# The shared expert of the two-choice stage, two batches to a product

## The chip, the cores and the metric

The kernel runs on one core of a Trainium2 chip. The metric is the device time of one execution, in microseconds. A core has five engines that run their own instruction streams and meet at semaphores: PE (TensorE, matmuls into PSUM; PEld is its loading of weights), ACT (ScalarE), DVE (VectorE), POOL (GpSimd) and SP, which here only issues DMAs. PSUM has eight banks, each of 128 partitions by 512 float32 values.

## What is computed

The program is a chain of attention and feed-forward layers, each followed by a layer norm, on 8 batches of 256 tokens of 128 values. The change lies in one of them: a mixture of eight experts of which each token takes two, beside a shared expert that all tokens go through. From the reference, cut:

```python
# x: (8, 256, 128); eight routed experts of inner width 512, a shared one of 1024
xg = xf[dispatch]                                   # each expert's tokens, at most 320
gate = silu(einsum('ech,ehi->eci', xg, rg)); up = einsum('ech,ehi->eci', xg, ru)
eout = einsum('eci,eih->ech', gate * up, rd)
routed = zeros_like(xf).at[dispatch.reshape(-1)].add(contrib.reshape(-1, h))
shared = jax.nn.silu(x @ sg) * (x @ su) @ sd
return shared + SCALE * routed.reshape(b, s, h)
# and around it: x = layernorm(x + that)
```

## The kernel before

The stage is `stage_top2_experts`, L2543. Constants: `B` is 8 batches, `L` 256 tokens a batch, `TPB` 2 tiles of 128 tokens a batch, `NT` 16 tiles in all, `SC` 8 chunks of 128 hidden columns of the shared expert, `FC` 4 chunks of a routed expert, `E2` 8 experts, `C2` 320 places each.

Order of the stage. DVE works out the routing. POOL then issues 32 indirect DMAs (L2830) that scatter the token rows into slots in memory; when all have landed, SP loads the slots (L2846) and PE turns them (L2628). While this goes on, PE, ACT and DVE compute the first half of the shared expert, batches 0 to 3. Next come the eight routed experts; their results are stored, and POOL issues 32 indirect DMAs (L2838) that gather two rows per token. Meanwhile the engines compute the second half of the shared expert, batches 4 to 7, and DVE combines, batch by batch, the two gathered rows and the shared result (`combine`, L2779 to L2788), then normalises (L2799). At the end PE turns the tokens again (L2649) and ACT writes them to `xT` (L2685).

One batch of the shared expert goes chunk by chunk. PE computes the gate product (`sg`) and the up product (`su`) of 256 tokens, L2618; in float32 each product is two matmul records. ACT takes the silu of the gate (L2674), DVE multiplies it with the up product into `shared_hid` (L2762). Gate products alternate between banks 3 and 4, up products between 5 and 6, so PE may be two chunks ahead of DVE; chunks 0 and 1 of a batch wait for the last product of DVE of the batch before. After chunk 1 of batch i PE computes the down products of batch i-1 (L2609: 8 chunks for each of two tiles, and L2610, which adds `x` by a product with the identity) into bank 7; 18 products, 36 matmul records. ACT copies bank 7 to `shared` (L2666, `keep_shared`) behind its silu of chunk 1. The last batch of a half has its down products at the end of the half.

The order of work on each engine is the order in which the code is written. The first half's last copy is what the turning of the slots waits behind, on ACT; the second half's last copy is what the last `combine` waits for.

## Time and profile before

| | us |
|---|---|
| median of 3 runs | 1851.13 (1848.86 to 1851.44) |
| profiled execution | 1853.07 |
| its span | 1851.2 |
| PE busy | 1537.6 (83%) |
| DVE busy | 1013.3 (55%) |
| ACT busy | 868.2 (47%) |
| POOL busy | 632.8 (34%) |

The page also cuts the span in 40 slices of 46.3 us and gives the busy share of each engine in each, and the clock that was granted to PE. The stage of this document lies in slices 31 to 36, from about 1384 to 1629 us. Times in the rows count from the start of the span. In a row of the timeline, the square brackets hold how long the engine had been idle before it, and what ended that. A row of PE shows when the matmul started, while its semaphore is raised when it has ended.

### The profile page before, as it was taken

The page shows a single profiled execution, that of the slowest core. Times are in us where ns is not written, and L with a number is a line of the kernel's source. Part 1 is how long each engine was busy: PE and PEld are TensorE (multiplying, and loading weights), DVE is VectorE, ACT ScalarE, POOL GpSimd, SP SyncE. Part 2 cuts the span into 40 slices and gives each one's busy share as a digit, 9 for nine tenths or more (in the row PEclk, how much of TensorE's full clock was granted, in tenths as well). Part 3 has the DMA queues.
Part 4 walks back from the last instruction along what each step waited for, and adds up shares of the span by engine and source line. Part 5 has one row for each costly group of instructions (what it writes and reads, how often), then busy time and mean ns, then how long its engine had stood idle before and what let it go on. Part 6 is the DMA issues. An engine that isn't in the chain of part 4 may idle for free. (4 is left out here: it accounts for less than half of the span.)

```text
span 1851.2 us, 31581 instructions
## 1 busy us (share of the span) xinstructions
PE 1537.6 (83%) x11326; PEld 1136.8 (61%) x11327; DVE 1013.3 (55%) x2402; ACT 868.2 (47%) x1935; POOL 632.8 (34%) x707
## 2 busy tenths in 40 slices
PE   4689977899787999995669999999974895668996
PEld 3356664566573577764647878787763774535664
DVE  6565546665376799982245553566452221344555
ACT  5556544555357777752434444444441231235553
POOL 3487513976132577753210001000036005111113
PEclk8799988899896899996869999999986898869998
DMA  7300000000002444706160000000001102100000
GB/s 221 102 13 12 12 7 3 12 18 12 7 1 38 80 75 78 79 22 165 42 186 1 1 1 1 1 1 0 1 1 46 29 19 46 11 4 2 2 2 24
DMA packets 75277, 63.71 MB, mean 34 GB/s; under 512 B 25367, under 2 KB 62790, under 8 KB 75142
## 3 DMA queue, kind: packets, MB, share of 16 engines
q1 hardware_dynamic: 65142, 53.53, 13.0%
q0 software_dynamic: 3072, 6.30, 1.7%
q10 hardware_dynamic: 6928, 2.12, 0.5%
q8 instruction: 81, 1.33, 0.3%
q14 instruction: 54, 0.44, 0.1%
HBM read 48.09 MB, written 9.57 MB: 31 GB/s over the span
## 5 line engine op out<-in xcount | busy, mean ns | idle before, releaser
L1354 POOL TENSOR_TENSOR inject<-delta_x,b_rows 128x512 f32<-128x512 f32 x128 | 159.6, 1270 | 82.7 <-DVE delta_x L1604 42.2
L1625 DVE TENSOR_TENSOR_SCAN state<-bank,inject 128x512 f32<-128x512 f32 x128 | 150.4, 1206 | 5.0 <-ACT bank L1535 4.7
L2058 POOL TENSOR_TENSOR ve<-mv,eps 128x1 f32<-128x1 f32 x32 | 6.1, 190 | 341.3 <-DVE mv L2206 341.3
L1535 ACT ACTIVATE bank<-delta,a_neg 128x255 f32<-128x255 f32 x256 | 109.0, 472 | 11.9 <-DVE state L1625 11.4
L3313 DVE TENSOR_REDUCE top<-bank 128x2 f32<-128x512 f32 (+1 forms) x96 | 61.8, 686 | 72.4 <-PE bank L3015 51.5
L2167 ACT ACTIVATE Z<-bank 128x512 f32<-128x512 f32 x64 | 34.7, 595 | 129.4 <-PE bank L2120 129.4
L2762 DVE TENSOR_TENSOR shared_hid<-shared_gate,bank 128x256 f32<-128x256 f32 x64 | 26.5, 421 | 124.9 <-ACT shared_gate L2674 72.6
L2144 ACT ACTIVATE U<-bank 128x512 f32<-128x512 f32 x128 | 74.6, 593 | 40.3 <-PE bank L2081 39.2
L2618 PE MATMUL bank<-xT,sg 128*128 128x256 f32 x128 | 45.3, 437 | 55.8 <-DVE shared_hid L2762 51.3
L594 POOL TENSOR_TENSOR rotated<-rot_cos,rot_sin 128x512 f32<-128x512 f32 x56 | 70.8, 1268 | 52.2 <-DVE rot_sin L900 52.2
L600 POOL TENSOR_TENSOR inv_norm<-sum_sq,neghalf 128x16 f32<-128x16 f32 x28 | 82.0, 2929 | 4.2 <-POOL sum_sq L598 0.2
L1440 PEld LDWEIGHTS bank<-tabs,by_token 128*128 128x128 f32 x512 | 67.5, 195 | 24.9 <-issue 15.0
L637 PE MATMUL bank<-wqkv,hT 128*128 128x512 f32 x128 | 69.1, 670 | 15.0 <-ACT hT L798 12.0
L1546 ACT ACTIVATE by_token<-bank,c_cols 128x256 f32<-128x256 f32 x128 | 53.6, 469 | 50.1 <-PE bank L1411 49.8
L1444 PE MATMUL bank<-x_work,tabs 128*128 128x512 f32 x128 | 73.7, 658 | 0.0
L3226 ACT ACTIVATE prob<-bank 128x384 f32<-128x384 f32 x128 | 53.2, 501 | 37.0 <-PE bank L3043 37.0
L1440 PE MATMUL bank<-tabs,by_token 128*128 128x128 f32 x512 | 68.9, 278 | 0.0
L2618 PEld LDWEIGHTS bank<-xT,sg 128*128 128x128 f32 x128 | 24.7, 214 | 68.2 <-DVE shared_hid L2762 56.6
L897 DVE TENSOR_TENSOR rot_cos<-bank,rope 128x512 f32<-128x512 f32 x64 | 43.8, 685 | 39.9 <-ACT squares L803 29.1
L803 ACT ACTIVATE squares<-bank 128x512 f32<-128x512 f32 x64 | 38.0, 598 | 43.4 <-PE bank L637 25.4
L605 POOL TENSOR_TENSOR rotated<-rotated,inv_norm 128x512 f32<-128x512 f32 x56 | 57.2, 1042 | 2.2
L825 ACT ACTIVATE prob<-bank 128x512 f32<-128x512 f32 x64 | 34.7, 595 | 44.6 <-PE bank L684 44.6
(564 smaller groups left out, 4205.1 us busy)
## 6 DMA issues: line engine op xcount, KB each, us to landing
b_rows<-b_rows_dram SPq DMA_DIRECT2D x32, 512.0 KB, 8.6
v<-v SPq DMA_DIRECT2D x32, 130.0 KB, 2.3
slots<-zero SPq DMA_DIRECT2D x10, 256.0 KB, 3.6
rows<-slots SPq DMA_DIRECT2D x10, 256.0 KB, 4.7
moe_w<-in_L_ffn_rg_dram SPq DMA_DIRECT2D x1, 2048.0 KB, 8.6
moe_w<-in_L_ffn_ru_dram SPq DMA_DIRECT2D x1, 2048.0 KB, 14.3
wqkv<-in_L_ffn_wqkv_dram SPq DMA_DIRECT2D x2, 768.0 KB
slots_out<-y SPq DMA_DIRECT2D x8, 160.0 KB, 2.1
```

The source lines that it names most:

```text
L594: pool.tensor_tensor(rot[:, p, m, :], rc[:, m % 2, :], rs[:, m % 2, :], ALU.add).then_inc(s.added.sem, 1)
L600: pool.tensor_tensor(flat(rn), flat(ss), net.neghalf[:, 0:2 * LH], ALU.pow).then_inc(s.inv_norm.sem, 2)
L605: pool.tensor_tensor(r, r, rn[:, m, :].unsqueeze(2).to_broadcast([P, LH, LDH]), ALU.mult).then_inc(s.roped.sem, 1)
L637: pe.matmul(to, hT[:, p, tok(t)], w[:, j * INNER:(j + 1) * INNER], start=True, stop=True).then_inc(s.qk_ps.sem, 1)
L1354: pool.tensor_tensor(dB[:, n % R, :, :], dx[:, :, seq(n)], both(b_all[:, q % 4, n % CH, :]), ALU.mult).then_inc(s.inject.sem, 1)
L1440: last = pe.matmul(sum_bank(i)[:, c * L + t * P:c * L + (t + 1) * P], hcT[:, j % RT, t, c * P:(c + 1) * P], ident, start=(k == 0 and t == ...
L1444: last = pe.matmul(sum_bank(i)[:, :], ident, flat(hc[:, j % R, :, :]), start=False, stop=(k == NS - 1))
L1535: last = act.activation(dA[n % RD][:, c, 1:L], delta[:, c, i * L + 1:(i + 1) * L], ACT.Exp, scale=a_neg[:, c, k:k + 1])
L1625: dve.tensor_tensor_scan(flat(h[:, n % R, :, :]), flat(dA[n % RD]), flat(dB[:, n % R, :, :]), 0.0, ALU.mult, ALU.add).then_inc(s.state.sem, 1)
L2144: act.activation(U[:, m % 2, 4 * (g - 1):4 * g, :], bank[n % 2][:, :].rearrange("p (h t) -> p h t", h=4), ACT.Copy)\
L2618: pe.matmul(to[:, 0:L], w[:, c * P:(c + 1) * P], net.xT[:, i * L:(i + 1) * L], start=True, stop=True).then_inc(done.sem, 1)
L3313: dve.tensor_reduce(to, M[u % 2].rearrange("p (c k) -> p c k", c=count), AX.X, ALU.max).then_inc(s.maxed.sem, 1)
```

## The change

The shared expert is computed by pairs of batches. A gate or up product takes 512 tokens, and fills a whole bank; ACT and DVE treat 512 columns in an instruction. `shared_gate` and `shared_hid` are twice as wide. The down products of a pair are computed together, after chunk 1 of the next pair: the even batch's into bank 0, the odd one's into bank 7, and ACT copies both one after the other. DVE no longer runs `combine` between single batches but three of them behind the first pair of the second half and four behind the second. A wait is added ahead of the turning of the slots, since that writes bank 0 too.

```diff
-        sgate, shid = sb("shared_gate", [P, 2, L]), sb("shared_hid", [P, 2, SC, L])
+        sgate, shid = sb("shared_gate", [P, 2, 2 * L]), sb("shared_hid", [P, 2, SC, 2 * L])
...
+            shared_bank = lambda i: bank[7 * (i % 2)]
...
-                def shared_down(i):
-                    pe.wait_ge(s.s_hid.sem, s.s_hid.at(i, SC))
-                    pe.wait_ge(s.shared.sem, s.shared.at(i, 0))
-                    for t in range(TPB):
-                        tok = slice(t * P, (t + 1) * P)
-                        for c in range(SC):
-                            pe.matmul(bank[7][:, tok], shid[:, i % 2, c, tok], net.sd[:, c, :], start=(c == 0), stop=False)
-                        last = pe.matmul(bank[7][:, tok], net.xT[:, i * L + t * P:i * L + (t + 1) * P], net.tab("ident"), start=False, stop=True)
-                    last.then_inc(s.shared_ps.sem, 1)
+                def shared_down(p):
+                    pe.wait_ge(s.s_hid.sem, s.s_hid.at(p, SC))
+                    for i in (2 * p, 2 * p + 1):
+                        if i >= 2:
+                            pe.wait_ge(s.shared.sem, s.shared.at(i - 1, 0))
+                        for t in range(TPB):
+                            tok, at = slice(t * P, (t + 1) * P), i % 2 * L + t * P
+                            for c in range(SC):
+                                pe.matmul(shared_bank(i)[:, tok], shid[:, p % 2, c, at:at + P], net.sd[:, c, :], start=(c == 0), stop=False)
+                            last = pe.matmul(shared_bank(i)[:, tok], net.xT[:, i * L + t * P:i * L + (t + 1) * P], net.tab("ident"), start=False, stop=True)
+                        last.then_inc(s.shared_ps.sem, 1)
...
-                                pe.matmul(to[:, 0:L], w[:, c * P:(c + 1) * P], net.xT[:, i * L:(i + 1) * L], start=True, stop=True).then_inc(done.sem, 1)
+                                pe.matmul(to[:, :], w[:, c * P:(c + 1) * P], net.xT[:, 2 * i * L:2 * (i + 1) * L], start=True, stop=True).then_inc(done.sem, 1)
...
-                shared_expert(0, HALF)
+                shared_expert(0, PAIRS // 2)
+                pe.wait_ge(s.shared.sem, s.shared.at(PAIRS - 2, 1))
...
-                            act.activation(sgate[:, c % 2, :], gate_bank(c)[:, 0:L], ACT.Silu).then_inc(s.s_silu.sem, 1)
+                            act.activation(sgate[:, c % 2, :], gate_bank(c)[:, :], ACT.Silu).then_inc(s.s_silu.sem, 1)
                             if c == 1 and i > first:
-                                keep_shared(i - 1)
+                                keep_shared(2 * i - 2)
+                                keep_shared(2 * i - 1)
...
-                dve.tensor_tensor(shid[:, i % 2, c, :], sgate[:, c % 2, :], up_bank(c)[:, 0:L], ALU.mult).then_inc(s.s_hid.sem, 1)
+                dve.tensor_tensor(shid[:, i % 2, c, :], sgate[:, c % 2, :], up_bank(c)[:, :], ALU.mult).then_inc(s.s_hid.sem, 1)
```

On PE, around the first down products of the first half. Before, the down products of batch 0 stand behind chunk 1 of batch 1, and chunk 2 of batch 1 follows:

```order
L2618 MATMUL bank4<-xT,sg 128x256
L2618 MATMUL bank6<-xT,su 128x256
L2609 MATMUL bank7<-sd,shared_hid_246 128x128 x8
L2610 MATMUL bank7<-tabs,xT 128x128
L2609 MATMUL bank7<-sd,shared_hid_246 128x128 x8
L2610 MATMUL bank7<-tabs,xT 128x128
L2618 MATMUL bank3<-xT,sg 128x256
L2618 MATMUL bank5<-xT,su 128x256
```

With the change, chunk 1 of pair 1 is followed by the down products of batches 0 and 1:

```order
L2621 MATMUL bank4<-xT,sg 128x512
L2621 MATMUL bank6<-xT,su 128x512
L2612 MATMUL bank0<-sd,shared_hid_246 128x128 x8
L2613 MATMUL bank0<-tabs,xT 128x128
L2612 MATMUL bank0<-sd,shared_hid_246 128x128 x8
L2613 MATMUL bank0<-tabs,xT 128x128
L2612 MATMUL bank7<-sd,shared_hid_246 128x128 x8
L2613 MATMUL bank7<-tabs,xT 128x128
L2612 MATMUL bank7<-sd,shared_hid_246 128x128 x8
L2613 MATMUL bank7<-tabs,xT 128x128
L2621 MATMUL bank3<-xT,sg 128x512
```

Half as many gate and up products stand ahead of the first down products for the same tokens, and twice as many down products stand together.

On ACT, the first half; `shared_gate` is written by the silu, `shared` by `keep_shared`:

```order
-L2674 ACTIVATE shared_gate<-bank 128x256 x10
-L2666 ACTIVATE shared<-bank 128x256
-L2674 ACTIVATE shared_gate<-bank 128x256 x8
-L2666 ACTIVATE shared<-bank 128x256
-L2674 ACTIVATE shared_gate<-bank 128x256 x8
-L2666 ACTIVATE shared<-bank 128x256
-L2674 ACTIVATE shared_gate<-bank 128x256 x6
-L2666 ACTIVATE shared<-bank 128x256
```

```order
+L2678 ACTIVATE shared_gate<-bank 128x512 x10
+L2670 ACTIVATE shared<-bank 128x256 x2
+L2678 ACTIVATE shared_gate<-bank 128x512 x6
+L2670 ACTIVATE shared<-bank 128x256 x2
```

The first copy stands behind ten silus as before, but these are of pairs now, so it stands behind 5120 columns instead of 2560.

## Rows read from the trace of the kernel before

**Rows 1.** Stretches: us, busy us (instructions) of each engine, PE's clock, DMA share, GB/s.

```profile
1409.00:1440.00 31.00, 6.84 (x18) 3.49 (x17) 0.78 (x3) 0.94 (x3) 18.99 (x20) 0.59 0.25 77
1440.00:1445.00 5.00, 4.88 (x12) 3.89 (x13) 1.24 (x4) 0.97 (x3) 0.00 (x0) 0.50 0.21 60
...
1549.00:1586.00 37.00, 4.37 (x30) 3.54 (x28) 0.34 (x2) 0.19 (x1) 23.65 (x26) 0.62 0.41 46
```

**Rows 2.** Timeline of POOL, first and last scatter and gather: start, us, line, operation [idle].

```profile
1393.57 1.07 POOL L2830 DMA_INDIRECT slots<-x_tok,scatter  x1 [4.98 <-DVEq L2742]
...
1432.83 0.96 POOL L2830 DMA_INDIRECT slots<-x_tok,scatter  x1 [0.30 <-issue]
1540.59 0.98 POOL L2838 DMA_INDIRECT y_first<-slots_out,gather  x1 [106.80 <-DMA slots_out<-y]
...
1579.33 0.94 POOL L2838 DMA_INDIRECT y_second<-slots_out,gather  x1 [0.30 <-issue]
```

**Rows 3.** Timeline of ACT, silus of batch 1, and the copies behind both holes.

```profile
1404.99 0.38 ACT L2674 ACTIVATE shared_gate<-bank 128x256 f32<-128x256 f32 x1 [1.53 <-PE bank L2618]
1407.14 0.38 ACT L2674 ACTIVATE shared_gate<-bank 128x256 f32<-128x256 f32 x1 [1.77 <-issue]
1438.95 0.38 ACT L2666 ACTIVATE shared<-bank 128x256 f32<-128x256 f32 x1 [31.43 <-remote]
...
1585.81 0.38 ACT L2666 ACTIVATE shared<-bank 128x256 f32<-128x256 f32 x1 [38.46 <-remote]
```

**Rows 4.** Timeline of PE in the first half, 1405 to 1428 us.

```profile
1405.92 1.95 PE L2609 MATMUL bank<-sd,shared_hid 128*128 128x128 f32 x16
...
1411.35 0.27 PE L2609 MATMUL bank<-sd,shared_hid 128*128 128x128 f32 x1 [1.63 <-issue]
...
1414.18 0.29 PE L2610 MATMUL bank<-tabs,xT 128*128 128x128 f32 x1 [1.63 <-issue]
...
1427.57 0.59 PE L2618 MATMUL bank<-xT,su 128*128 128x256 f32 x1 [1.51 <-issue]
```

**Rows 5.** Timeline of PE in the second half, the last down products of batch 4.

```profile
1551.00 0.39 PE L2610 MATMUL bank<-tabs,xT 128*128 128x128 f32 x2
```

**Rows 6.** Timeline of ACT and PE in the stage of one-choice experts, during its scatters.

```profile
868.81 0.60 ACT L1808 ACTIVATE la_k<-bank 128x512 f32<-128x512 f32 x1 [6.47 <-remote]
...
870.94 2.66 PE L1793 MATMUL bank<-la_p,y 64*128 64x128 f32 x14 [0.34 <-issue]
```

**Rows 7.** Timeline of ACT, the last copy of each half.

```profile
1474.68 0.38 ACT L2666 ACTIVATE shared<-bank 128x256 f32<-128x256 f32 x1 [4.90 <-PE bank L2610]
...
1621.48 0.38 ACT L2666 ACTIVATE shared<-bank 128x256 f32<-128x256 f32 x1 [0.72 <-PE bank L2610]
```

**Rows 8.** Timeline of PE in steady state, batches 2 and 3.

```profile
1448.66 1.95 PE L2609 MATMUL bank<-sd,shared_hid 128*128 128x128 f32 x16
...
1452.68 0.60 PE L2618 MATMUL bank<-xT,sg 128*128 128x256 f32 x2
...
1457.43 0.59 PE L2618 MATMUL bank<-xT,su 128*128 128x256 f32 x2
1458.59 0.70 PE L2618 MATMUL bank<-xT,sg 128*128 128x256 f32 x2 [0.57 <-DVE shared_hid L2762]
```

**Rows 9.** Durations in ns (min/median/max) of PE, and groups by form: busy us, mean ns.

```profile
L637 PE MATMUL bank<-wqkv,hT x60: 592/592/1192, 61.1 to 194.4; 128*128 128x512 f32 x60
...
L2618 PE MATMUL bank<-xT,sg x128: 376/379/797, 1389.9 to 1615.8; 128*128 128x256 f32 x128
...
L897 DVE TENSOR_TENSOR rot_cos<-bank,rope 128x512 f32<-128x512 f32 x64 | 43.8, 685 | 39.9 <-ACT squares L803 29.1
...
L825 ACT ACTIVATE prob<-bank 128x512 f32<-128x512 f32 x64 | 34.7, 595 | 44.6 <-PE bank L684 44.6
```

**Rows 10.** Timeline of DVE, the first normalisation of the stage's end.

```profile
1621.07 2.14 DVE L2799 TENSOR_SCALAR y_second<-y_first,n_mv,n_rstd 128x128 f32<-128x128 f32 x8
```

**Rows 11.** DMA queues from 1402 to 1404 us: packets, MB, share of the engines' time.

```profile
q8 instruction: 1, 0.02, 3.1%
```

More of the change, by code:

```diff
@@ L2564, in stage_top2_experts @@
         SC = IS // P
-        sgate, shid = sb("shared_gate", [P, 2, L]), sb("shared_hid", [P, 2, SC, L])
+        sgate, shid = sb("shared_gate", [P, 2, 2 * L]), sb("shared_hid", [P, 2, SC, 2 * L])
         shared = sb("shared", [P, NT, D])
-        HALF, EARLY = B // 2, B - 1
+        PAIRS, EARLY = B // 2, B - 1
         MS = [(0, P), (P, P), (2 * P, C2 - 2 * P)]
@@ L2642, in _ @@
                 pe.wait_ge(s.y_sb.sem, s.y_sb.at(0, E2))
-                shared_expert(HALF, B)
+                shared_expert(PAIRS // 2, PAIRS)
                 for i in range(B):
@@ L2665, in keep_shared @@
                     act.wait_ge(s.shared_ps.sem, s.shared_ps.at(i, 1))
-                    act.activation(shared[:, TPB * i:TPB * (i + 1), :], bank[7][:, 0:L].rearrange("p (t d) -> p t d", d=D), ACT.Copy)\
+                    act.activation(shared[:, TPB * i:TPB * (i + 1), :], shared_bank(i)[:, 0:L].rearrange("p (t d) -> p t d", d=D), ACT.Copy)\
                         .then_inc(s.shared.sem, 1)
@@ L2685, in update @@
                     act.activation(net.xT[:, i * L:(i + 1) * L], bank[1 + i % 2][:, 0:L], ACT.Identity).then_inc(s.x_updated.sem, 1)
-                shared_expert(0, HALF)
-                keep_shared(HALF - 1)
+                shared_expert(0, PAIRS // 2)
+                keep_shared(PAIRS - 2)
+                keep_shared(PAIRS - 1)
                 for g in range(KT // 4):
@@ L2701, in _ @@
                 copy_y(act, E2 - 1)
-                shared_expert(HALF, B)
+                shared_expert(PAIRS // 2, PAIRS)
+                keep_shared(B - 2)
                 deviation(0, 0, EARLY)
@@ L2754, in _, with shared_pair @@
                 weights()
-                def shared_batch(i):
+                def shared_pair(i):
                     for c in range(SC):
@@ L2760, in shared_batch @@
                         if i >= 2:
-                            dve.wait_ge(s.shared_ps.sem, s.shared_ps.at(i - 1, 0))
-                        dve.tensor_tensor(shid[:, i % 2, c, :], sgate[:, c % 2, :], up_bank(c)[:, 0:L], ALU.mult).then_inc(s.s_hid.sem, 1)
-                for i in range(HALF):
-                    shared_batch(i)
+                            dve.wait_ge(s.shared_ps.sem, s.shared_ps.at(2 * (i - 1), 0))
+                        dve.tensor_tensor(shid[:, i % 2, c, :], sgate[:, c % 2, :], up_bank(c)[:, :], ALU.mult).then_inc(s.s_hid.sem, 1)
+                for i in range(PAIRS // 2):
+                    shared_pair(i)
                 for e in range(E2):
@@ L2800, in normalise @@
                     last.then_inc(s.xn_ready.sem, 1)
-                shared_batch(HALF)
-                combine(0)
-                shared_batch(HALF + 1)
-                combine(1)
-                combine(2)
-                shared_batch(HALF + 2)
-                combine(3)
-                combine(4)
-                shared_batch(HALF + 3)
-                combine(5)
-                combine(6)
+                shared_pair(PAIRS // 2)
+                for i in range(3):
+                    combine(i)
+                shared_pair(PAIRS // 2 + 1)
+                for i in range(3, EARLY):
+                    combine(i)
                 inverse(0, 0, EARLY)
```

## The prediction

> **What bounds the kernel now.** I read the page first: PE is busy for 83% of the span, but the fortieths between about 1410 and 1435 us and between about 1550 and 1585 us are almost empty on PE, and both lie in the stage that the change edits. The table of stretches then gives the size of the two holes: 6.84 us of PE work in 31 us, and 4.37 us in 37 us, on a granted clock of 0.59 and 0.62 [rows 1]. Third I asked who works in them. It is POOL alone, with its indirect DMAs: the 32 scatters run from 1393.57 to 1433.8 us, the 32 gathers from 1540.59 to 1580.3 us [rows 2]. Fourth, the timelines of ACT and PE show what waits. In the first half PE ran the down products of batch 0 from 1405.92 on, at full pace; then, from 1411.35, one matmul in one or two microseconds, the last of that group at 1414.18, and after the gate and up products of chunks 2 and 3 of batch 1 it stopped at 1427.57 [rows 4]. ACT waits for exactly the semaphore of the matmul at 1414.18 (its copy of bank 7, line 2666), and gets it at 1438.95 [rows 3]: 24 us late. In the second half the matmul that ACT waits for starts at 1551.00 [rows 5], and ACT gets the signal at 1585.81 [rows 3]. The profile calls the releaser "remote", since the matmul had ended long before. So while POOL issues indirect DMAs, PE's signals arrive late and PE itself is slowed. The first routed stage shows the same at another place: PE is back at full pace at 870.94, when its 16 scatters are over, and ACT's wait before it reads "remote" too, 6.47 us long [rows 6].
>
> I call this the hold, and its end the release: 1438.95 and 1585.81 us, 5.2 and 5.5 us after the last indirect DMA was issued. What each half is worth is then what is left after the release, up to ACT's last copy at 1474.68 and at 1621.48 [rows 7]: 35.7 us in both halves. Everything before the release is hidden under POOL's DMAs, and everything after it is on the path, since routed experts follow the first half and the last normalisation the second.
>
> **The pieces, part by part.** A chunk is one of the 8 pieces of 128 hidden columns. (1) Products. In steady state six chunks of a batch run from 1452.68 to 1457.43, start to start 0.43 us for a gate or up product of 256 columns, so 0.86 a chunk [rows 8]. Each product is two matmul records; a record of 512 columns takes 592 ns where one of 256 takes 379 [rows 9], 213 ns more, as much as the 215 ns pace. So a chunk of a pair costs 1.72 us, and two batches cost PE what they did: half as many matmuls, no time saved in the stream. (2) ACT and DVE per chunk: 0.60 and 0.69 us for 512 columns [rows 9], together 1.3, under the 1.72 of PE; both engines have cover, and their 32 saved instructions each are worth nothing on the path. (3) The gap at the end of a batch, where PE waits for the last product of DVE: its last pair of matmuls starts at 1457.43, the next possible start is 0.43 later, and the real one is at 1458.59 [rows 8]: 0.73 us. With 512 columns it grows by the longer DVE instruction, 0.27, to 1.0. Eight gaps of 0.73 become four of 1.0: 1.8 us saved in all. (4) Down products: 4.02 us a batch, 1448.66 to 1452.68 [rows 8]; unchanged in number, now two batches in a row, 8.04, into banks 0 and 7. PE's wait for ACT's copy of two batches ago is met long before. ACT copies both while PE goes on to chunk 2, whose first product needs 0.86 us; nothing waits. The new wait ahead of the transposes is for the copy of batch 2, four microseconds older than the end of the down products: free. (5) DVE combines batches 0, 1 and 2 after pair 2, three times 1.7 us, under 11 us of PE work; batches 3 to 6 after pair 3, 6.7 us under 8.04 of down products. The last normalisation started at 1621.07 [rows 10], 0.4 ahead of the last copy. Now four combines follow the last product of DVE, which ends 8.3 before that copy; 6.7 for them (eight short instructions each, taken at 1.7) and 0.7 for root and reciprocal make it start 0.9 ahead. Gain 0.5 us, between 0 and 1.
>
> Add the pieces up for before, as a test: resume 1.2, 20 chunks 17.2, three gaps 2.2, three downs 12.1, the last copy 0.2; and PE restarts at half clock, 0.50 over the first 5 us [rows 1], which costs 2.5. Sum 35.4 of 35.7: the model holds, 0.3 unexplained.
>
> **Where the gain comes from.** The order of PE's work against the hold changes. Before, the release finds done: batch 0, chunks 0 to 3 of batch 1, one batch of down products. After, PE starts pair 0 at 1389.9, as now, without the idle time at 1394 (its two chunks last until ACT's table load is over). Slow clock until some 1394.6, chunks 2 to 7 by 1407.1, chunks 0 and 1 of pair 1 by 1411.5, and only then the dense down products, 72 matmuls. In the second half pair 2 starts at 1537.6 as now; its chunks end at 1551.4, those of pair 3 that come first at 1555.7. In the hold PE got 33 of 36 down matmuls through at full pace and then 11 matmuls from 1411.35 to 1427.57, 0.68 a microsecond. Applied to 72: 33 by 1415, 13 more until 1434, 26 left over, 2.9 us; the second half the same within 0.2. Left after a release: 2.9 of down products, six chunks 10.3, one gap 1.0, two downs 8.0, copy 0.2, slow clock 2.5, the unexplained 0.3: 25.2 against 35.7. The change gains 10.5 us a half, 21.0, and 0.5 in the tail: **21.5 us**. In plain words: per matmul issued, PE gets twice the columns through before it is slowed, and what it does while slowed are down products that no one needs yet.
>
> Bounds of the unknown: how many of the 72 get through. None, if the hold stops PE at once: 8.0 left instead of 2.9, gain 5.4 a half. All: 0 left, gain 13.4 a half. Main case 1824 to 1841. I stay near the middle since the rate is one read in the same code under the same DMAs.
>
> The profiled execution took 1853.07 us for its span of 1851.2, and the median of the runs is 1851.13; the differences above are taken from the median: 1851.1 - 21.5 = 1829.6, **1830 us**.
>
> **Rivals.** (a) The hold strikes early and hard. In the first half ACT's start at 1404.99 is the last on time; that of 1407.14 stood 1.77 us [rows 3]. The changed kernel is then in chunk 6 of pair 0. If from there on no signal at all arrived, PE would run chunks 6 and 7 and stop; left are the last products of DVE 1.4, chunks of pair 1 13.8, gap 1.0, downs 16.1, slow clock and copy 3.0: 35.3, and in the second half, held from 1547.4 in chunk 5, 37: no gain, **1850 us**. Against it: the signal for 1407.14 did come, within 2 us, and in the earlier stage one came 6.47 us late during the scatters [rows 6]; such delays would still let chunks 0 and 1 of the next pair through within 20 us. That puts it in the main range.
> The Trainium skill, page "SBUF — State Buffer", section "SBUF: two separate sides", says that DMA and engine ports are disjoint and that PE and ACT never wait on anyone. By that rule no transfer would hold PE and only the 1.8 us of gaps and the tail would be gained, 1849. The two holes of [rows 1] speak against it as an account of this kernel, or at least against its reach.
> (b) It is a matter of PE's instruction fetch. One block of instructions of queue 8, PE's by its pace, is fetched between 1402 and 1404 us [rows 11], one more between 1546 and 1549, just ahead of the slowing, and none in the holes. If the hold follows that fetch by some 3 us, it moves with PE's instruction count: in the first half to chunk 7 of pair 0, much as in the main case; in the second half, 128 instructions fewer having gone before, to about 1563, the end of the down products, with two chunks of pair 3 behind them: 2.9 and two chunks 3.4 less left, 6.3 more gained: **1823 us**.
> The Trainium skill, "Runtime: NRT & Kernel Launch", section "Instruction fetch mechanics", has blocks of 256 instructions, fetched ahead and mostly hidden. The earlier stage agrees with hidden: it slows with no block of that queue in its 25 us.
> (c) Slower. A chunk is now twice as large and two batches of down products stand behind chunk 1. If the hold acts on the signals already from the first landings of the DMAs, so that fewer than six chunks of each pair are through at the release, every chunk short of that costs 1.72 us over (a). Break-even is six; at four in both halves it is 3.4 twice over: **1857 us**. For it: DVE's wait and PE's are now at twice the distance. Against it: signals are punctual for 10 us after the first scatter [rows 2, 3].
> (d) The hold, which needs dense matmuls, forms late or not at all: nothing then keeps the first half from ending at about 1445, when the rows are in; up to 30 us each. **1810 us** or less.
>
> **Chances.** Main case 0.58, (a) 0.16, (b) 0.08, (c) 0.10, (d) 0.08. The range 1819 to 1852 takes in the main case, (b) and (a), and leaves out (c) and (d), 0.18. About 0.2% or 3.7 us is what a measurement of this kernel tells from no change. Faster: main, (b), (d) and a fifth of (a), 0.77. Same: the rest of (a), 0.12. Slower: (c) and a bit of (a), 0.11.
>
> **What would show it.** The stretch from the release to ACT's last copy should shrink from 35.7 to about 25 us in both halves, the release staying 5.2 to 5.5 us after the last indirect DMA (PE's clock 0.5 for 5 us behind it). The first matmul of chunk 0 of pair 1 should start near 1408, and down products should fill the hold. L2621 should show 512 columns at 592 ns when warm. Wrong would be: "remote" waits on the gate copies of pair 0 (then (a) or (c)), an even pace through the down products (then (d)), a hold that starts in the second half only after 1560 (then (b)).

## The result, and the profile after

The kernel after takes 1827.25 us (1826.17 to 1828.55, 4 runs), the kernel before 1850.61 (1848.86 to 1851.44, 4 runs): a ratio of 0.988, interval 0.986 to 0.989, or 23.4 us less. The profiled execution of after has a span of 1825.7 us. Forecast were 1830 us, 1819 to 1852.

Did the gain come from the place I gave? The stretches of after, to be held against [rows 1]: us, busy us (instructions) of PE, PEld, DVE, ACT and POOL, PE's clock, DMA share, GB/s.

```profile
1412.00:1440.00 28.00, 9.53 (x45) 8.13 (x44) 0.00 (x0) 0.38 (x1) 15.35 (x17) 0.58 0.28 87
1440.00:1445.00 5.00, 5.00 (x23) 3.26 (x23) 0.69 (x1) 1.47 (x3) 0.00 (x0) 0.95 0.00 0
1545.00:1577.00 32.00, 10.38 (x48) 9.39 (x48) 1.65 (x5) 0.38 (x1) 16.90 (x18) 0.57 0.42 39
1577.00:1582.00 5.00, 5.00 (x18) 2.61 (x17) 1.38 (x2) 1.58 (x3) 0.00 (x0) 1.00 0.00 0
```

Both holes are still there, on the same low clock. The 5 us stretches behind them read 0.95 and 1.00, where before had 0.50 [rows 1], but they begin 2.8 and 4.6 us behind the release, and that of before 1.1 us behind its own. In the first 5 us counted from the release itself the clock is 0.67 and 0.54 in after, and 0.50 twice in before. ACT's timeline shows the release and the last copy of each half:

```profile
1409.55 0.60 ACT L2678 ACTIVATE shared_gate<-bank 128x512 f32<-128x512 f32 x1 [1.12 <-issue]
1437.19 0.38 ACT L2670 ACTIVATE shared<-bank 128x256 f32<-128x256 f32 x1 [27.05 <-remote]
...
1461.39 0.38 ACT L2670 ACTIVATE shared<-bank 128x256 f32<-128x256 f32 x1 [3.64 <-PE bank L2613]
...
1572.36 0.38 ACT L2670 ACTIVATE shared<-bank 128x256 f32<-128x256 f32 x1 [29.70 <-remote]
...
1597.21 0.38 ACT L2670 ACTIVATE shared<-bank 128x256 f32<-128x256 f32 x1 [1.44 <-PE bank L2613]
```

From release to last copy it is 24.2 and 24.85 us, where before had 35.7 twice [rows 3, 7]. POOL's last indirect DMAs in after:

```profile
1431.27 0.96 POOL L2832 DMA_INDIRECT slots<-x_tok,scatter  x1 [0.30 <-issue]
...
1566.13 0.95 POOL L2840 DMA_INDIRECT y_second<-slots_out,gather  x1 [0.30 <-issue]
```

The releases stand 5.0 and 5.3 us behind their ends; before had 5.2 and 5.5. And PE through the first hole:

```profile
1406.67 1.12 PE L2621 MATMUL bank<-xT,sg 128*128 128x512 f32 x2 [0.85 <-DVE shared_hid L2769]
...
1410.20 1.95 PE L2612 MATMUL bank<-sd,shared_hid 128*128 128x128 f32 x16
...
1414.57 0.27 PE L2612 MATMUL bank<-sd,shared_hid 128*128 128x128 f32 x1 [0.52 <-issue]
1415.98 0.27 PE L2613 MATMUL bank<-tabs,xT 128*128 128x128 f32 x1 [1.14 <-issue]
...
1436.28 0.37 PE L2612 MATMUL bank<-sd,shared_hid 128*128 128x128 f32 x1 [1.04 <-issue]
1436.98 1.85 PE L2612 MATMUL bank<-sd,shared_hid 128*128 128x128 f32 x7 [0.33 <-issue]
...
1441.73 0.59 PE L2621 MATMUL bank<-xT,sg 128*128 128x512 f32 x1
```

Pair 0 is through, chunks 0 and 1 of pair 1 as well, and it is the down products of pair 0 that are held, from 1414.57 on one matmul in one to three microseconds. From 1436.98 on follow 7, 2, 16 and 2 of them, 27 of 72.

### The profile page after: what moved, and what is told of

Its sections match the earlier page's. It is cut to its first block and busy times, and to the rows that moved or that the text cites. A ratio compares the mean times of both kernels' runs of the same rounds, so it can differ in the third digit from the quotient of the medians.

```text
span 1825.7 us, 31193 instructions
## 1 busy us (share of the span) xinstructions
PE 1532.5 (84%) x11199; PEld 1118.1 (61%) x11199; DVE 1008.7 (55%) x2370; ACT 864.1 (47%) x1903; POOL 632.7 (35%) x707
## 5 line engine op out<-in xcount | busy, mean ns | idle before, releaser
L1535 ACT ACTIVATE bank<-delta,a_neg 128x255 f32<-128x255 f32 x256 | 109.0, 472 | 13.2 <-DVE state L1625 12.7
L2769 DVE TENSOR_TENSOR shared_hid<-shared_gate,bank 128x512 f32<-128x512 f32 x32 | 21.8, 687 | 102.1 <-PE bank L2621 63.3
L2612 PE MATMUL bank<-sd,shared_hid 128*128 128x128 f32 x256 | 39.8, 302 | 35.9 <-issue 34.2
L2612 PEld LDWEIGHTS bank<-sd,shared_hid 128*128 128x128 f32 x256 | 36.8, 218 | 40.6 <-issue 37.2
```

The costliest lines, as they stand in the source:

```text
L1535: last = act.activation(dA[n % RD][:, c, 1:L], delta[:, c, i * L + 1:(i + 1) * L], ACT.Exp, scale=a_neg[:, c, k:k + 1])
L2612: pe.matmul(shared_bank(i)[:, tok], shid[:, p % 2, c, at:at + P], net.sd[:, c, :], start=(c == 0), stop=False)
```

## Experiments

The first four ran on one chip and changed the question, so they are told together. One measure serves for all: the time from the start of the first silu of the shared expert to the start of the last copy of its second half, from ACT's timeline. For the kernel before it is 1621.48 - 1395.38 = 226.1 us, for after 1597.21 - 1393.81 = 203.4. It leaves out the rest of the program, which differs from one execution to the next by several microseconds.

### The first four: there is no hold on this chip

**Down products last.** The chunks of both pairs come first, then all down products of a half, and ACT's copies move with them (not shown):

```diff
-                            if c == 1 and i > first:
-                                shared_down(i - 1)
-                    shared_down(end - 1)
+                    for i in range(first, end):
+                        shared_down(i)
```

> The kernel after, with the down products moved behind all chunks of a half: PE runs the 16 chunks of both pairs first, then the down products of both pairs (144 matmul records in a row); ACT copies all four results then. Nothing is left out.
>
> Theory 1, the hold needs a dense row of short matmuls while POOL issues indirect DMAs. The chunks of pair 1 then run at full pace under the DMAs: pair 1 ends 8 times 1.72 behind 1406.67, so the down products start near 1421.3, not 1410.20, and only they are held. In the kernel after 4.2 us went at full pace (some 36 records) and the crawl gave 0.68 a microsecond: 36 and 8 are through at the release at 1437, 100 left, 11.1 us, and 1 to 2.5 for the slow clock: last copy near 1450 (after: 1461.39). Second half: chunks from 1524.3 to 1557.2, 100 records left at 1572.4, last copy near 1586 counted without the gain of the first half (after: 1597.21). Gain 11 to 12 us a half, 1804 us in all.
>
> Theory 2, the hold comes a fixed time after the first indirect DMA (some 22 us in the first half), or where PE's instructions are fetched, whatever PE does. Then PE is held from 1414.6 on in chunk 5 of pair 1, three chunks and all down products are left at the release, 24.5 us again: 1827 us, as the kernel after, and remote waits on gate copies.

**Order alone.** After, with products of 256 columns:

```diff
-                                pe.matmul(to[:, :], ..., net.xT[:, 2 * i * L:2 * (i + 1) * L], ...).then_inc(done.sem, 1)
+                                for h in range(2):
+                                    last = pe.matmul(to[:, h * L:(h + 1) * L], ..., net.xT[:, (2 * i + h) * L:(2 * i + h + 1) * L], ...)
+                                last.then_inc(done.sem, 1)
```

> The kernel after, with every gate and up product of 512 columns made as two of 256, one signal for both. Order, banks, ACT and DVE as in the kernel after: this is the change without its wide products on PE.
>
> Theory 1, the gain comes from the order (16 chunks' worth of columns ahead of the dense down products of a pair) and PE's stream costs the same, 4 times 0.43 a chunk: within 2 us of the kernel after, 1827, the hold again setting in some 4 us after the first down product.
>
> Theory 2, the gain comes from the number of PE's instructions (twice the columns per matmul before the hold strikes): with 256 columns the hold should strike where it did before in terms of matmuls, in pair 0, and the gain of 23 us be mostly lost: 1840 to 1850 us.

**Direct DMAs** in after and in before:

```diff
-                        pool.indirect_dma_start(net.slots[1], ..., net.x_tok[:, t * P:(t + 1) * P], None).then_inc(moved, 16)
+                    sp.dma_start(net.slots[1][t * P:(t + 1) * P, :], net.x_tok[:, t * P:(t + 1) * P]).then_inc(moved, 16)
...
-                            pool.indirect_dma_start(to[:, t, :], None, net.slots_out[1], ...).then_inc(arrived[i], 16)
+                            sp.dma_start(to[:, t, :], net.slots_out[1][t * P:(t + 1) * P, :]).then_inc(arrived[i], 16)
```

> The kernel after without any indirect DMA in this stage: in place of 32 scatters SP issues 16 direct DMAs of the same rows to slots in order of tokens, in place of 32 gathers 32 direct DMAs of 128 rows each. So the routing is left out of the result (the wrong rows are moved), engines do the same work.
>
> Theory 1, the hold is made by the indirect DMAs that POOL issues: there is none now. First half: start 1388.4, 16 chunks 27.5, two gaps 1.7, down products 16.1, slow clock 2.5, copy 0.2: last copy near 1436 (after: 1461.39). Second half the same 48 us behind its start instead of 73. Gain 25 a half, 1777 us, and the down products at an even pace of 4.02 us a batch.
>
> Theory 2, it is made by transfers that read and write SBUF while PE runs dense matmuls, whoever issues them: remote waits of several microseconds remain while they move, over 1785 us.

> The kernel before, with the same replacement: direct DMAs by SP in place of scatters and gathers; the routing is left out of the result.
>
> This is the price of the change itself without a hold. By the pieces of the prediction: start 1389.9, 32 chunks of 0.86, four gaps of 0.73, four downs of 4.02, slow clock 2.5, copy 0.2: 49.2 us a half instead of 84.8 and 83.9; so 70 us less than the kernel before, 1781 us. The kernel after in this form should then be faster by 1.8 (gaps) and 0.5 (tail), some 1.5 us more for its earlier start of the first half, 2 to 4 us in all. If the wide products bring more of their own, the difference between the two is larger than 4 us.

Measured, in this order: 1767.6, 1764.9, 1763.6 and 1771.8 us, none near what was expected. But the kernel before, run beside them, took 1770.5 us (28 runs, 1768 to 1781) and not 1850.6. Nothing was to be learned of the hold from a chip that has none: before with direct DMAs is no faster than before itself (ratio 1.000, 0.998 to 1.002). The two with direct DMAs differ by 8.1 us, where 2 to 4 were expected. What the four do tell is the price of the change without a hold; that follows below.

**After and before again**, both unchanged:

> The kernel after once more, unchanged, beside the kernel before. On the chip of the first four experiments the kernel before took 1770.5 us instead of 1850.6, and no wait of the shared expert was remote.
>
> Theory A, the hold is a property of the chip (or of its state on a day), not of the kernel: there are two results of this change. Where a chip shows the hold (before near 1850) this kernel is 23 us faster, 1827. Where it doesn't (before near 1770), the first half of the shared expert still takes about 4 us less, as 44.46 against 48.68 us from the first silu to the last copy in the two kernels without indirect DMAs, and the second half as much: 8 us less, near 1763.
>
> Theory B, the direct DMAs did take a hold away and the kernel before was fast for another reason: this kernel then differs from the kernel of 256 columns in the same order (1764.89 us) by more than 5 us on such a chip.

> The kernel before once more, unchanged, for its trace on this chip. Theory A: if its time is near 1770, the two holes of the shared expert are gone although POOL issues the same 32 scatters and 32 gathers in about 40 us each, the down products take 4.02 us a batch, and the first half lasts 48 to 49 us from the first silu to the last copy instead of 84.8 behind PE's start; if near 1850, remote waits of over 20 us as before. Theory B: a near 1770 time with holes, the gain being elsewhere in the program.

Another chip, again without a hold: before 1772.35, after 1765.55, ratio 0.9966 (0.9953 to 0.9978); theory A had put after near 1763. Here is the first hole's stretch in the trace of before on that chip:

```profile
1409.00:1440.00 31.00, 28.96 (x172) 24.20 (x171) 8.38 (x19) 10.89 (x26) 6.71 (x7) 1.00 0.20 60
```

and ACT's last copy of each half:

```profile
1427.63 0.38 ACT L2666 ACTIVATE shared<-bank 128x256 f32<-128x256 f32 x1 [4.90 <-PE bank L2610]
...
1537.93 0.38 ACT L2666 ACTIVATE shared<-bank 128x256 f32<-128x256 f32 x1 [0.72 <-PE bank L2610]
```

The same kernel, the same 32 scatters from 1377.52 on, 1.26 us apart as before: PE is busy for 28.96 of 31 us at full clock, no wait is remote, and it is 158.6 us from the first silu to the last copy, not 226.1. So theory A stands: the hold belongs to the chip, or to something that goes with it, and not to the kernel. The spans differ by 84.0 us (1851.2 and 1767.2); 67.5 of them lie in this stage. The stage of one-choice experts shows it too: from its first scatter to its first gather it is 65 to 67 us in the five traces with the hold and 54 to 60 in the nine without. The runs of this study fell on five chips: two with the hold (before at 1852.0 and 1853.6), three without (1770.1 to 1772.4; one of them at two times, both without). One more difference stands in the lists of DMA issues, here of before in 1370 to 1480 us with the hold:

```profile
slots<-x_tok,scatter POOLq DMA_INDIRECT x32
```

and on the chip without it, where the profile knows when they landed (2.2 us, median):

```profile
slots<-x_tok,scatter POOLq DMA_INDIRECT x32, 2.2
```

### What the change is worth without a hold

From first silu to last copy, in the traces of these chips: before 158.6, and with direct DMAs 158.6 as well; after 153.7; order alone 154.1 (two more executions: 154.3 and 154.0); down products last 162.4. The change brings 4.9 us there, and order alone 4.5 of them. In the first half it is 48.30 against 44.08 us, in the second 46.61 against 44.89; some 1 us is given back between them.

Of the second half's 1.7 us, 0.43 lies in the measure: its first silu stands 1.17 us behind PE's first product of 512 columns, and 0.74 behind one of 256. The gaps are four in each half of before (three between batches, one ahead of the last down products) and two in after. In before each costs 0.84 us, 0.73 of waiting and 0.11 by which the first product behind it is slower; in after 1.10. That makes 1.16 us a half.

Between the halves 0.4 of the 1.0 us is the same effect of the measure. The other 0.6 is lost where PE turns the slots: in after PE gets there sooner and has to wait for the rows (0.22 us at 1437.68, for `rows<-slots`), in before it doesn't. So on such a chip the first half has come down to the time that the scatters need.

The first half has 2.5 us more than the second, 3.1 more than its gaps explain. I suspected the clock.

**Before with a warm PE**: three products that no one reads, while PE waits for ACT's table load.

```diff
+                            if c == 1 and i == 0:
+                                for _ in range(3):
+                                    pe.matmul(bank[7][:, 0:L], net.sg[:, 0:P], net.xT[:, 0:L], start=True, stop=True)
```

> The kernel before, with three more products of 256 columns into the unused bank 7 behind chunk 1 of batch 0, where PE stood idle for 2.68 us (it waits for ACT, which loads a table). The results of these three are never read.
>
> Without a hold, as on the last two chips, the first half took 48.68 us from the first silu to the last copy, the kernel after 44.46, while in the second half it was 46.99 against 45.27. The excess of the first half, 2.5 us, is by my reading PE's clock: before restarts behind an idle time and gets the full clock at 1384.6, 10.9 us behind its first product; the kernel after has two chunks of twice the work there, keeps PE busy and has the full clock 4.4 us behind its first. If that is so, this kernel has the full clock some 4 to 6 us behind its first product, and its first half takes 46.5 to 47.3 us, 1.5 to 2 less. If instead the wide products are what saves the 2.5 us, the first half stays at 48.7 or, if the extra products delay chunk 2, above it. With a hold nothing changes: 1850 us.

This came to a chip with the hold, so the first half as a whole says nothing, and the time did not change: 226.1 us from first silu to last copy, as before, 1849.8 us in all. But the start can be read. This kernel's stretch from 1395 to 1400 us, and its silu of chunk 6:

```profile
1395.00:1400.00 5.00, 4.58 (x21) 3.78 (x22) 2.39 (x6) 2.05 (x6) 3.78 (x5) 1.00 0.17 56
```

```profile
1399.61 0.38 ACT L2677 ACTIVATE shared_gate<-bank 128x256 f32<-128x256 f32 x1 [0.48 <-issue]
```

The same two of before, on a chip with the hold too:

```profile
1395.00:1400.00 5.00, 3.67 (x11) 2.95 (x12) 1.77 (x5) 1.79 (x5) 3.78 (x4) 0.72 0.15 52
```

```profile
1402.21 0.38 ACT L2674 ACTIVATE shared_gate<-bank 128x256 f32<-128x256 f32 x1 [0.48 <-issue]
```

The clock is 1.00 instead of 0.72, and the silu of chunk 6 starts 5.14 us behind the first (1394.47) instead of 6.83 (1395.38): 1.7 us, without a wide product. So 1.7 of the 3.1 us is the clock. The change gets this since two chunks of a pair keep PE busy where two of a batch leave it idle for 2.68 us; in after it is idle for 1.1.

Most of the rest is work done ahead. When PE resumes behind the table load, it has two chunks of 256 columns behind it in before and two of 512 in after, 1.72 us of products more, and it resumes 0.47 us later behind the first silu (1.43 against 0.96, both without a hold): 1.25 us. Gaps 1.16, clock 1.7 and this 1.25 make 4.1 of the first half's 4.2 us. The 1.25 is worked out from the timelines, no run isolates it.

### Down products and combines last, with and without a hold

In the kernel with the down products last, the second half was slower than after's (50.17 us against 44.89): three combines of DVE, 4.9 us of work and 1.3 of waiting for a gather, stood between the chunks of pair 2 and those of pair 3, with no down products to cover them. Another 4.5 us were lost between the halves, in part where PE waited 1.43 us for the rows. All seven combines went behind pair 3:

```diff
                 shared_pair(PAIRS // 2)
-                for i in range(3):
-                    combine(i)
                 shared_pair(PAIRS // 2 + 1)
-                for i in range(3, EARLY):
+                for i in range(EARLY):
                     combine(i)
```

> The kernel with all down products of a half behind its chunks, and now also all seven combines of DVE behind the last pair. In the kernel with the down products last, DVE stood at the combine of batch 2 for rows that the gathers had not brought yet, and two chunks of pair 3 started 5.62 and 2.82 us late on ACT; in total 6.2 us. Nothing is left out.
>
> Without a hold: 6 us less in the second half than that kernel, and, against the kernel after, one wait of PE for DVE less in each half (1.1 us): 1761 to 1762 us where before takes 1770. With a hold: theory 1 of that kernel (the hold needs dense short matmuls) gives 1804 us, theory 2 (it comes whatever PE does) 1825 to 1827.

> The kernel with all down products of a half behind its chunks and all combines behind the last pair, once more on another chip. The first two chips gave no hold, so that the question on the hold stayed open. If this chip shows it (before near 1850): by theory 1 (the hold needs a dense row of short matmuls) 1804 us, by theory 2 (it comes whatever PE does) 1825 to 1827. If it doesn't: the stage again 2.2 us shorter than in the kernel after, 43.34 and 44.17 us for the halves.

Without a hold: 1766.0 us, ratio to before 0.9955 (0.9935 to 0.9975), 153.2 us from first silu to last copy against 153.7 of after. Expected were 1761 to 1762 us; in the medians it is no faster than after (1765.55). With the hold: 1821.56 us where before took 1852.02, one execution each; 195.9 against 203.4 us of after, 7.5 less. Neither 1804 nor 1827. Why, ACT's silus of pair 1 show (chunk 1 first):

```profile
1410.78 0.60 ACT L2677 ACTIVATE shared_gate<-bank 128x512 f32<-128x512 f32 x1 [1.12 <-issue]
1415.11 0.60 ACT L2677 ACTIVATE shared_gate<-bank 128x512 f32<-128x512 f32 x1 [3.74 <-PE bank L2621]
1422.81 0.60 ACT L2677 ACTIVATE shared_gate<-bank 128x512 f32<-128x512 f32 x1 [7.10 <-PE bank L2621]
1431.91 0.60 ACT L2677 ACTIVATE shared_gate<-bank 128x512 f32<-128x512 f32 x1 [8.51 <-remote]
1438.24 0.60 ACT L2677 ACTIVATE shared_gate<-bank 128x512 f32<-128x512 f32 x1 [5.73 <-remote]
...
1459.43 0.39 ACT L2669 ACTIVATE shared<-bank 128x256 f32<-128x256 f32 x1 [3.64 <-PE bank L2613]
```

There is no short matmul anywhere near, and yet from chunk 2 on each signal comes later: the hold does not need dense matmuls, theory 1 falls. Nor does PE stand: a chunk is signalled every six to nine microseconds. That fits neither a switch that density throws nor one that time throws, so I counted. The stretch from the first indirect DMA to the last silu that starts on time, for the eight holds of four kernels; the instructions of PE and PEld are the first two counts in a row. Before, after, down products and combines last, order alone (a first half and a second each):

```profile
1393.57:1404.99 11.42, 8.12 (x29) 6.31 (x29) 4.41 (x14) 4.46 (x11) 8.74 (x9) 0.84 0.14 48
1540.59:1546.97 6.38, 5.81 (x27) 4.58 (x26) 2.58 (x7) 2.30 (x6) 4.86 (x6) 1.00 0.18 44
```

```profile
1392.01:1409.55 17.54, 15.60 (x36) 6.51 (x35) 7.22 (x15) 6.77 (x12) 13.54 (x14) 0.98 0.15 50
1527.30:1542.06 14.76, 13.92 (x33) 6.00 (x32) 7.75 (x21) 4.70 (x9) 11.41 (x12) 1.00 0.19 49
```

```profile
1393.24:1410.78 17.54, 15.59 (x36) 6.51 (x35) 7.22 (x15) 6.76 (x12) 13.56 (x14) 0.98 0.15 50
1525.34:1540.10 14.76, 13.93 (x33) 6.00 (x32) 5.49 (x8) 4.70 (x9) 11.40 (x12) 1.00 0.19 49
```

```profile
1400.57:1406.70 6.13, 4.99 (x22) 4.05 (x21) 3.10 (x9) 3.18 (x5) 4.91 (x5) 0.96 0.14 45
1543.55:1550.39 6.84, 6.84 (x33) 6.03 (x32) 2.75 (x4) 2.32 (x4) 5.32 (x6) 1.00 0.18 45
```

In time these stretches last 6.1 to 17.5 us, a factor of three. In PE instructions they are 58, 53, 71, 65, 71, 65, 43 and 65. The number of instructions is the nearer rule, though not an exact one. Three of the eight are lower bounds: in both halves of after and in the second of before, the next signal that one can watch is that of a whole row of down products, some 72 instructions later.

PE's own pace gives a sharper count. In before and after PE issues at full pace up to 1409.70 and 1552.60 us, and up to 1414.05 and 1546.50. From the first indirect DMA to there it is 129, 135, 139 and 133 PE instructions, in 16.1, 12.0, 22.0 and 19.2 us. So with the hold PE gets through some 130 to 140 instructions behind the first indirect DMA before it is slowed itself, whatever time they take. In the first half of before, where both can be read, its signals fall behind some 70 instructions sooner. From then on it is about one PE instruction a microsecond: a down matmul with its weights every 1.4 to 2.8 us in after, a chunk of 8 instructions in six to nine here.

### Order or width, with the hold

The kernel of order alone was run until it met the hold:

> The kernel after with every 512 column product made as two of 256, once more on another chip, to have it where the hold shows. The trace of the kernel with its down products last, on a chip with the hold, gives a new reading: PE's signals are on time for the first 65 to 75 PE instructions (weight loads and matmuls) behind the first indirect DMA, whether this takes 12 us or 18, then they come late at about one instruction a microsecond until the indirect DMAs are over, and PE can run some 60 instructions ahead of them.
>
> Theory N, the number of instructions counts, so the wide product is the gain. A chunk of a pair is 16 instructions here, not 8: 4 chunks of pair 0 are signalled on time, 1.5 more in the remaining 24 us, 2 issued ahead. At the release about 9 chunks and all 16.1 us of down products are left: 9 times 1.72, 1.1, 16.1, copy and slow clock 3: 35 to 38 us, as before the change or worse. If the chip shows the hold (kernel before near 1851): 1848 to 1856 us.
>
> Theory O, the order (down products behind two batches of chunks) is the gain: 1827 to 1830 us.
>
> On a chip without the hold (before near 1770): 1765 us again, and nothing is told apart.

> The same kernel a third time (512 columns made as two products of 256, order as after), since the chips of the first two showed no hold.
>
> Theory N (PE's signals are on time for some 65 to 75 instructions behind the first indirect DMA, then about one a microsecond until the end): with a hold 1848 to 1856 us, no gain over the kernel before. Theory O (the order is the gain): 1827 to 1830 us. Without a hold: 1765 us and nothing told apart.

> The same kernel a last time (order as after, products of 256 columns). Theory N, number of PE instructions: with a hold 1848 to 1856 us. Theory O, order: 1827 to 1830 us. Without a hold (before near 1770) the question stays open.

On chips without a hold it took 1764.9, 1766.9 and 1772.2 us; with the hold 1845.82 us, one execution, where before took 1853.63 beside it. That lies in neither range. From first silu to last copy, which leaves out what the rest of the program adds, it is 212.9 us: 13.2 less than before, where after has 22.7. ACT's silus of chunks 3, 4, 6, 7 of pair 0 and of chunk 0 of pair 1, and the last copy of the half:

```profile
1406.70 0.60 ACT L2680 ACTIVATE shared_gate<-bank 128x512 f32<-128x512 f32 x1 [1.13 <-issue]
1409.15 0.60 ACT L2680 ACTIVATE shared_gate<-bank 128x512 f32<-128x512 f32 x1 [1.85 <-PE bank L2622]
...
1419.10 0.60 ACT L2680 ACTIVATE shared_gate<-bank 128x512 f32<-128x512 f32 x1 [6.48 <-remote]
1431.83 0.60 ACT L2680 ACTIVATE shared_gate<-bank 128x512 f32<-128x512 f32 x1 [12.14 <-issue]
1445.95 0.60 ACT L2680 ACTIVATE shared_gate<-bank 128x512 f32<-128x512 f32 x1 [13.53 <-PE bank L2622]
...
1477.64 0.39 ACT L2672 ACTIVATE shared<-bank 128x256 f32<-128x256 f32 x1 [3.64 <-PE bank L2613]
```

A chunk is now 16 PE instructions and not 8. The signals are late from chunk 4 of pair 0 on, where after, with the hold too, had all of pair 0 and two chunks of pair 1 on time; from chunk 6 on they are 7 to 14 us apart, where the kernel above, with half the instructions, had them 6 to 9 apart. The signals are as many in both kernels, one for a product of 512 columns or for its two parts, so it is not their number. At the release eight chunks and all down products are left, 31.7 us up to the last copy (after: 24.2). The second half does better, 26.6 us from the release at 1588.68: six chunks of pair 2 are signalled on time there, not four, and PE got into the down products of pair 2. So both theories hold in part: of the 22.7 us the order brings 13.2, and the half number of instructions the other 9.5.

The sum hides that the halves differ. From first silu to last copy the first half is 79.3 us in before, 75.3 with order alone and 67.6 in after: the order brings 4.0 of 11.7 us. The second half is 83.1, 73.5 and 71.7: there it brings 9.6 of 11.4. What I call order is also a bundle: the down products stand behind two batches of chunks, and with one signal for 512 columns PE may be twice as much work ahead of DVE. The two were not run apart, nor was width without the order, and with the hold each of these kernels has one trace, not all on the same chip. That the measure repeats, before with three more products shows: 226.1 us, like before.

## Why the prediction was right, and where not

The time (1830 against 1827.25) and the place were right. In part that was luck: the result was measured where the hold is, like the trace that I had read, and nothing in the prediction says that another chip would give 7 us and not 23. The halves brought 11.5 and 10.8 us and the tail 0.7, 23.0 in all where 21.5 was forecast. The terms:

- **Left after the release.** Forecast 25.2 us in each half; 24.2 and 24.85 measured. Matmuls left: 26 forecast, 27 and 28 found. That it fits so well is luck too: while slowed, PE got 0.54 and 0.44 matmuls a microsecond through and not 0.68, but for longer, until 1436.98 and 1572.15 and not until the last indirect DMA. In before 32 down matmuls went at full pace, not 33. The terms in it: chunks 1.72 us (forecast 1.72), down products 4.02 a batch (4.02), the gap 0.28 longer (0.27; PE's idle time is 0.85 in the row of 1406.67 above against 0.57 in [rows 8]). Each gap was put 0.11 us too low, by the slower first product behind it, in before as in after. The record of 512 columns lasts 592 ns, as in [rows 9]; here PE's durations (min/median/max) in after:

```profile
L2621 PE MATMUL bank<-xT,sg x64: 592/592/1163, 1388.4 to 1586.6; 128*128 128x512 f32 x64
```

  Chunk 0 of pair 1 was forecast near 1408 us and came at 1406.67, in an execution whose stage starts 1.56 us earlier (PE's first product at 1388.37, before 1389.92).
- **The slow clock** was a little too dear. I put 2.5 us behind the left-over down products. It lies in them: 27 took 4.75 us instead of 3.0, so 1.75 (28 took 5.4 in the second half instead of 3.1, so 2.3), and the chunks behind had the full clock.
- **The tail** was forecast at 0.5 us, the last normalisation 0.9 ahead of the last copy. It is 1.14 ahead (1596.07 and 1597.21), 0.7 gained.
- **Rivals (a) and (c)**, a hold that stops the chunks of pair 0, did not come true in after: its last signal on time is that of chunk 1 of pair 1. But remote waits on gate copies of pair 0 are what the kernel of order alone shows, with its twice as many PE instructions in the chunks, so they were nearer than I had them.
- **Rival (b), PE's instruction fetch**, fell. The DMA queues of after from 1519 to 1525 us have this row, and none of queue 8 from 1524.5 to 1546.9, while the hold begins behind 1542: some 20 us apart, where in before they were a few.

```profile
q8 instruction: 1, 0.02, 1.4%
```

- **Rival (d) and the words "which needs dense matmuls"** fell with the kernel that has none there. Its time, 1810, was not reached by any kernel run with the hold (1821.56 at best). The step that failed is that I read a cause into where the slow matmuls stood: in before they stood in the down products since PE came to its 130th instruction behind the first scatter there.
- **"In plain words: per matmul issued, PE gets twice the columns through before it is slowed"** held, and is 9.5 of the 22.7 us, 7.7 of them in the first half. The second half of that sentence, that PE does while slowed what no one needs yet, is not what counts: the kernel that keeps the chunks in the hold and has its down products behind it is 7.5 us faster than after. An estimate from [rows 8] says why: at full pace a chunk of 8 instructions is 1.72 us of work, 0.21 an instruction, and a batch of down products is 4.02 us in 72 instructions, 0.06 each. While one instruction passes in a microsecond, the long ones save more.
- **The largest error** is in no term. The hold was real in the one trace that I read, but I took it for a property of the kernel. On three of five chips it is missing, before takes 1771 us, and the change gains 6.8 us by the medians (ratio 0.9966; 4.9 in its own stretch) and not 23. By the terms of the prediction it would have been 2.3: 1.8 for gaps, 0.5 for the tail. The gaps bring 2.3 and not 1.8; what the sum lacked is the start of the first half, 1.7 us of clock and 1.25 of work done ahead under the table load. I had written that the idle time there is gone, and priced it at nothing, since the hold covered it.

On three chips 64 indirect DMAs cost PE nothing (158.6 us with them and with direct ones). On the two others, and in the first trace, PE's signals are late by up to 24 us in the first half and 34 in the second (the matmul of 1551.00 [rows 5], signalled at 1585.81 [rows 3]). The Trainium skill, page "SBUF — State Buffer", section "SBUF: two separate sides", says that engine ports and DMA ports are disjoint and that PE never waits on anyone there. The traces of the three chips agree. Whether the late signals of the others have to do with these ports at all, no run shows, so they do not refute it.

What separates the chips stays open, and so does what fills or blocks. That the indirect DMAs cause the hold was not shown by an experiment, since the kernels with direct DMAs never met a chip that has it; for it speaks that all releases come 3 to 5.5 us behind the last one. One rival was not tested: every timed execution here, with the hold or without, was recorded by the profiler, and with the hold the record of this stage lacks the landings of these DMAs. Whether there is a hold when nothing is recorded, the runs do not say.

## What to carry to other kernels

A wait put down to "remote", for an engine that had long been done, can be the chip's: run the kernel before on another chip before reasoning from such a hole, and state a gain for both. Where the hold exists, count PE instructions from the first indirect DMA on: products with many columns belong ahead of it and into it, rows of short ones behind it. Without a hold the same change pays by fewer ends of batches and by a PE that is kept busy through another engine's table load, as it then has more work behind it and gets its full clock earlier, and the gain ends where the scattered rows come in.

## What I had not expected of the hardware

- The same kernel takes 1850.6 or 1770.5 us, by the chip; within either group the medians agree to 0.2%.
- With the hold, PE's signals are on time for 43 to 71 PE instructions behind the first of 32 indirect DMAs (eight cases, three of them lower bounds), and PE's own issue is at full pace for 129 to 139 (four cases, 12 to 22 us). Then a chunk of 8 instructions is signalled in six to eleven microseconds, and all is well 3 to 5.5 us behind the last.
- PE runs ahead of its own late signals: in after it had issued the 71st when its last signal on time arrived, and 36 down matmuls with their weights more until 1417.4, whose signal came at 1437.19, 19 us late.
- Three products that no one reads brought the full clock early enough to have chunk 6 1.7 us sooner.
